# Routing three batches of a mixture-of-experts layer in one pass instead of one batch at a time

## What is computed

```python
scores = sigmoid(x @ gate_weight.T)                    # 16 experts a token
biased = scores + expert_bias
group_scores = top_k(biased.reshape(T, 4, 4), 2).sum(-1)
_, gidx = top_k(group_scores, 2)                       # two of four groups stay
masked = where(group stays, biased, -inf)
_, sel = top_k(masked, 4)                              # four experts a token
w = take(scores, sel); w = w / (w.sum() + 1e-20) * 2.5
```

## Time and profile before

| | |
|---|---|
| runs | 1627.82 us median of 3 (1627.33 to 1629.36) |
| profiled execution | 1630.42 us, of it the span of the engines 1628.7 us |
| busy | TensorE 1290.0 us (79%), VectorE 1448.2 (89%), ScalarE 858.0 (53%), GpSimd 877.7 (54%) |
| instructions | 14027 in all, 1484 on VectorE |
| mean granted clock of TensorE | 0.907 of full |
| DMA | 264 MB, mean 162 GB/s |

### The profile page before, as it was taken

How to read it: one execution, slowest core, us unless ns; L and a number is a source line. 1 busy time by engine, 2 the same in 40 slices (tenths; PEclk the granted TensorE clock), 3 DMA queues, 4 the chain that set the end, 5 groups by cost and what they waited for, 6 DMA issues and landing times.

```text
span 1628.7 us, 14027 instructions
## 1 busy us (share of the span) xinstructions
PE 1290.0 (79%) x4244; PEld 710.4 (44%) x4244; DVE 1448.2 (89%) x1484; ACT 858.0 (53%) x1362; POOL 877.7 (54%) x449
## 2 busy tenths in 40 slices
PE   6785786888689868987869998799886998705778
PEld 2321332433244324442527576466664666503444
DVE  4899989999999999998897999999899999957884
ACT  5754647563755475444854765457564444414441
POOL 0467656645655565550464456755567665566521
PEclk8898799899989998998979999899999999957889
DMA  7354444434543454350366677686776777664421
GB/s 243 97 136 118 110 121 136 139 75 132 136 125 78 130 129 116 89 156 28 95 177 201 224 256 274 205 238 232 272 245 210 273 266 269 200 178 118 134 78 52
DMA packets 99836, 264.28 MB, mean 162 GB/s; under 512 B 10832, under 2 KB 11344, under 8 KB 93616
## 3 DMA queue, kind: packets, MB, share of 16 engines
q1 hardware_dynamic: 87936, 225.36, 47.0%
q0 software_dynamic: 11440, 37.50, 6.9%
q10 hardware_dynamic: 384, 0.52, 0.1%
HBM read 233.73 MB, written 29.62 MB: 162 GB/s over the span
## 4 chain that ended last, share of the span: by engine, by line
DVE 23%; PE 17%; issue 9%; DMA 6%; ACT 5%; POOL 4%; SPq 0%; DVEq 0%; ACTq 0%; POOLq 0%
PE banks L1109 7%; DVE state L1606 7%; DVE banks L1598 5%; DMA ys_d<-expert_out 3%; PE banks L1120 3%; DMA expert_w<-in_moe_w 2%; POOL state L442 2%; DVE x_res L1785 2%; DVE y_scan L1617 2%; PE banks L1029 1%; PE banks L1076 1%; DVE du L1327 1%; DVE small L1379 1%; PE banks L1257 1%; PE banks L1088 1%
## 5 line engine op out<-in xcount | busy, mean ns | idle before, releaser
L442 POOL TENSOR_TENSOR state<-state,bc_rows 128x1024 f32<-128x1024 f32 x256 | 606.5, 2370 | 620.8 <-DVE banks L1598 620.6
L1029 PE MATMUL banks<-state,ident 128*128 128x512 f32 x640 | 356.6, 691 | 132.7 <-POOL state L442 132.4
L1606 DVE TENSOR_TENSOR_SCAN state<-decay,banks 128x1024 f32<-128x1024 f32 x176 | 402.1, 2285 | 15.5 <-PE banks L1029 10.8
L1598 DVE TENSOR_TENSOR banks<-du,bc_rows 128x1024 f32<-128x1024 f32 x256 | 352.4, 1377 | 14.8 <-DVE state L1606 0.6
L1109 PE MATMUL banks<-z_gate,expert_w 128*128 128x256 f32 (+1 forms) x1504 | 287.2, 349 | 10.0 <-DMA expert_w<-in_moe_w 6.2
L1109 PEld LDWEIGHTS banks<-z_gate,expert_w 128*128 128x128 f32 x1504 | 250.8, 192 | 65.3 <-issue 24.3
L684 ACT ACTIVATE decay<-delta,neg_a 128x511 f32<-128x511 f32 x352 | 231.5, 713 | 89.0 <-DVE state L1606 77.7
L1029 PEld LDWEIGHTS banks<-state,ident 128*128 128x128 f32 x640 | 125.7, 212 | 335.2 <-POOL state L442 218.3
L1606 DVE TENSOR_TENSOR_SCAN state<-expert_w,banks 128x1024 f32<-128x1024 f32 x80 | 182.9, 2286 | 7.9 <-ACT expert_w L684 5.2
L1120 PE MATMUL banks<-expert_w,hidden 128*128 128x512 f32 x316 | 157.4, 614 | 3.1 <-DVE hidden L1627 3.1
L1617 DVE TENSOR_TENSOR y_scan<-y_scan,state 128x1024 f32<-128x1024 f32 x96 | 136.3, 1420 | 11.8 <-POOL state L442 11.6
(11 more groups left out here) (253 smaller groups left out, 1718.8 us busy)
## 6 DMA issues: line engine op xcount, KB each, us to landing
bc_rows<-bc_d SPq DMA_DIRECT2D x208, 512.0 KB
expert_w<-in_moe_w SPq DMA_DIRECT2D x48, 1536.0 KB, 9.2
ys_d<-expert_out SPq DMA_DIRECT2D x32, 512.0 KB, 10.2
ctx_t<-in_ctxT SPq DMA_DIRECT2D x8, 512.0 KB, 6.6
x_res<-in_x SPq DMA_DIRECT2D x4, 1024.0 KB, 10.7
xn_d<-y_scan SPq DMA_DIRECT2D x4, 1024.0 KB, 7.4
ys_d<-expert_out SPq DMA_DIRECT2D x15, 256.0 KB, 9.6
out_x<-x_res SPq DMA_DIRECT2D x3, 1024.0 KB, 4.4
```

The source lines that it names most:

```text
L442: nc.gpsimd.tensor_tensor(W[:, c % 4], W[:, c % 4], bcast2(BC[:, u, 1, :]), ALU.mult).then_inc(mulc_done, 1)
L1029: mm = nc.tensor.matmul(PS[:, m], ID[:, :], W[:, c % 4, m, :], start=False, stop=True, skip_group_check=True)
L1598: nc.vector.tensor_tensor(drive(s), DU[:, s % 2, 2 * h:2 * h + 2, :], bcast2(BC[:, u, 0, :]), ALU.mult).then_inc(mulb_done, 1)
L1606: nc.vector.tensor_tensor_scan(flat(W[:, c % 4]), flat(DAS[c % da_slots(s, i)]), flat(drive(s)), 0.0, ALU.mult, ALU.add).then_inc(scan_don ...
```

## The change

Batches 0, 1 and 2 are no longer routed one each in stages 1, 2 and 3. They are routed together in stage 3, at the place where batch 2 was routed, on rows of 3 x 64 = 192 columns. Batch 3 is routed where it was.

- `route_exp` writes its result into the batch's part of the weights' tile `CW`, where it waits; the tile `SC` is gone, and `route` computes the weights in place.
- `route(b0, b1, work, rank1, rank2)` takes a range of batches and its work area. For the three batches this is 7 rows of 192 columns in `ZS[:, 0:3]`, the ranks in halves of `ZS[:, 3]`; for batch 3 it is `SM`, `T1` and `T2` as before. It counts `ranked` up by the number of batches.
- Each operation is as it was with three times the columns; only `MAX8`, one for each token group, is issued 12 times instead of 4.
- In `mul_c` the flag `routed` is set for unit 5 of the last turn of stage 3 alone: in stages 1 and 2 multiply 5 waits for `mul_b` 6 again.
- `norm_bias(2 * s)` moves from behind unit 5 (behind the route) to behind unit 6, in all of stages 0 to 3.

```diff
-                routed = 1 <= s < NB and i == TURNS - 1 and c == 5 or s == NB and k + 1 == HS * NB + 2 * HPT
+                routed = s == NB - 1 and i == TURNS - 1 and c == 5 or s == NB and k + 1 == HS * NB + 2 * HPT
...
-                nc.scalar.activation(SC[:, :, :], AUX[0][:, 0:QT * NE].rearrange("p (q e) -> p q e", e=NE), ACT.Exp,
-                                     scale=-1.0).then_inc(sc_ready, 1)
+                nc.scalar.activation(CW[:, f * QT:(f + 1) * QT, :], AUX[0][:, 0:QT * NE].rearrange("p (q e) -> p q e", e=NE),
+                                     ACT.Exp, scale=-1.0).then_inc(sc_ready, 1)
...
-            def route(b):
-                q16 = lambda i: SM[:, i, :].rearrange("p (q e) -> p q e", e=NE)
-                dve.wait_ge(sc_ready, b + 1)
+            def route(b0, b1, work, rank1, rank2):
+
+                nq = QT * (b1 - b0)
+                n, gn = nq * NE, nq * NGRP
+                row = lambda i, m=n, at=0: work[:, i * n + at:i * n + at + m]
+                q16 = lambda i: row(i).rearrange("p (q e) -> p q e", e=NE)
+                sel, cw = (v[:, b0 * QT:b1 * QT, :] for v in (SEL, CW))
+                dve.wait_ge(sc_ready, b1)
                 dve.wait_ge(ld_small, 16 * 4)
 
-                link(nc.vector.tensor_scalar(SC[:, :, :], SC[:, :, :], 1.0, None, ALU.add))
-                link(nc.vector.reciprocal(SC[:, :, :], SC[:, :, :]))
+                link(nc.vector.tensor_scalar(cw, cw, 1.0, None, ALU.add))
+                link(nc.vector.reciprocal(cw, cw))
...
-                largest = SM[:, 1, 0:QT * 8].rearrange("p (q n) -> p q n", n=8)
-                for q in range(QT):
+
+                largest = row(1, nq * 8).rearrange("p (q n) -> p q n", n=8)
+                for q in range(nq):
                     ins = nc.vector.max(out=largest[:, q, :], in_=masked[:, q, :])
...
-                nc.vector.tensor_tensor(cw, cw, tot.unsqueeze(2).to_broadcast([P, QT, NE]), ALU.mult).then_inc(ranked, 1)
+                nc.vector.tensor_tensor(cw, cw, tot.unsqueeze(2).to_broadcast([P, nq, NE]), ALU.mult).then_inc(ranked, b1 - b0)
...
-                    if c == 5:
-                        if f >= 0:
-                            route(f)
+                    if c == 5 and s == NB - 1:
+
+                        route(0, s, flat(ZS[:, 0:3]), ZS[:, 3, 0:L // 2], ZS[:, 3, L // 2:])
+                    if c == 6:
                         norm_bias(2 * s)
                     if c == 6 and f >= 0:
                         shared_hidden(f, 0)
...
-            route(f)
+            route(f, s, flat(SM[:, :, :]), T1, T2)
```

More of the change, by code:

```diff
@@ L1410, in norm_bias, with rank_of @@
                                                op1=ALU.mult).then_inc(zn_ready, 1)
[L1412 to L1417, removed]
+            def rank_of(out, m, n, tri, s1, s2, nq=QT):
+                a = s1[:, 0:nq * n * n].rearrange("p (q e f) -> p q e f", q=nq, e=n)
+                c = s2[:, 0:nq * n * n].rearrange("p (q e f) -> p q e f", q=nq, e=n)
+                other = m.unsqueeze(2).to_broadcast([P, nq, n, n])
+                own = m.unsqueeze(3).to_broadcast([P, nq, n, n])
@@ L1418, in rank_of @@
                 nc.vector.tensor_tensor(a, other, own, ALU.is_gt)
                 link(nc.vector.tensor_tensor(c, other, own, ALU.is_equal))
-                link(nc.vector.tensor_tensor(c, c, tri.unsqueeze(1).to_broadcast([P, QT, n, n]), ALU.mult))
+                link(nc.vector.tensor_tensor(c, c, tri.unsqueeze(1).to_broadcast([P, nq, n, n]), ALU.mult))
                 link(nc.vector.tensor_tensor(a, a, c, ALU.add))
                 link(nc.vector.reduce_sum(out, a, AX.X))
-            def route(b):
-                q16 = lambda i: SM[:, i, :].rearrange("p (q e) -> p q e", e=NE)
-                dve.wait_ge(sc_ready, b + 1)
+            def route(b0, b1, work, rank1, rank2):
[5 more added lines that the diff above has]
+                dve.wait_ge(sc_ready, b1)
@@ L1435, in route @@
-                mx, mn = SM[:, 1, 0:32], SM[:, 2, 0:32]
+                link(nc.vector.tensor_tensor(biased, cw, EB[:, :].unsqueeze(1).to_broadcast([P, nq, NE]), ALU.add))
+                pairs = row(0).rearrange("p (n two) -> p n two", two=2)
+                mx, mn = row(1, n // 2), row(2, n // 2)
                 nc.vector.tensor_tensor(mx, pairs[:, :, 0], pairs[:, :, 1], ALU.max)
@@ L1438, in route @@
                 mxp, mnp = [v.rearrange("p (n two) -> p n two", two=2) for v in (mx, mn)]
-                top, lo, hi2 = SM[:, 3, 0:16], SM[:, 3, 16:32], SM[:, 3, 32:48]
+                top, lo, hi2 = row(3, gn), row(3, gn, gn), row(3, gn, 2 * gn)
                 nc.vector.tensor_tensor(top, mxp[:, :, 0], mxp[:, :, 1], ALU.max)
@@ L1467, in route @@
                 nc.vector.memset(starts[:, :, 0:1], 0.0)
-                many = SM[:, 1, 32:32 + QT]
+                many = row(1, nq, nq * 8)
                 link(nc.vector.reduce_sum(many, over, AX.X))
-                link(nc.vector.tensor_tensor_scan(SM[:, 5, :], SM[:, 4, :], SM[:, 3, :], 0.0, ALU.mult, ALU.add))
-                link(nc.vector.tensor_tensor(q16(5), q16(5), many.unsqueeze(2).to_broadcast([P, QT, NE]), ALU.add))
+                link(nc.vector.tensor_tensor_scan(row(5), row(4), row(3), 0.0, ALU.mult, ALU.add))
+                link(nc.vector.tensor_tensor(q16(5), q16(5), many.unsqueeze(2).to_broadcast([P, nq, NE]), ALU.add))
                 link(nc.vector.scalar_tensor_tensor(out=equal, in0=q16(5), scalar=float(TOPK), in1=equal, op0=ALU.is_le,
@@ L1474, in route @@
                 link(nc.vector.tensor_tensor(sel, over, equal, ALU.add))
-                link(nc.vector.tensor_tensor(cw, SC[:, :, :], sel, ALU.mult))
-                tot = SM[:, 6, 0:QT]
+                link(nc.vector.tensor_tensor(cw, cw, sel, ALU.mult))
+                tot = row(6, nq)
                 link(nc.vector.reduce_sum(tot, cw, AX.X))
```

19 lines of the change are left out of this document (7 added, 12 removed).

## The result

| | before | after |
|---|---|---|
| median of 6 runs each | 1629.47 us | 1616.12 us |
| lowest to highest | 1627.33 to 1631.12 | 1613.93 to 1621.30 |
| profiled execution, its span | 1630.42, 1628.7 | 1617.39, 1615.7 |
| busy share of VectorE, TensorE | 89%, 79% | 89%, 80% |

The ratio of the runs is 0.9923 (95% interval 0.9906 to 0.994): 12.5 us or 0.8% faster. The same kernel measured once more, on another chip, gave 0.9908 (0.9884 to 0.9932), 1616.51 us. Forecast were 1616.8 us and 11.0 us of gain.

The account below looks back on a forecast made before the run. VectorE (89% busy) was taken to set the pace inside a stage, TensorE's gaps behind VectorE's L1635 and its slow clock the transitions: -6.6 - 8.4 + 3.7 + 0.3 = -11.0 us, so 1616.8 us, range 1612.5 to 1622.

Parts of the forecast that it names:

- Stage 1, -6.6 forecast: Stage 1 to scan 4 of the next: TensorE gains gaps of 4.02 and 0.87 us and 1.7 us of slow L1068.
- stage 2, -8.4: Stage 2 to scan 4 of the next: TensorE gains its 5.40 us gap and 3.0 us of slow L1068.
- L1635 then needs the port ... ends at 322.9: Stage 1, VectorE: L1635 waits for GpSimd's multiply 5 and delta sum, ending at 322.9 instead of 332.4, gaining 9.5 us.
- VectorE waits 5.5 us at scan 4: Scan 4 behind stage 1: VectorE, ahead of TensorE, waits about 5.5 us instead of 2.58; 3.8 behind stage 2.
- rival (a): Stages 1 and 2: VectorE decides, not TensorE; both transitions give the whole 9.5 us, 1612.8 us in all; chance 0.07.
- ScalarE: Between route and scan 4: z_gate and taps come early enough, 3.8 us of cover; ScalarE as releaser would show the forecast wrong.
- Stage 3, route +3.7: Stage 3, VectorE: one route of 192 columns instead of 64 costs 3.7 us, all on the path to L1635.
- Stage 3, clock +0.3: Stage 3, TensorE: the slow stretch behind the longer gap costs 0.3 us more, range -0.4 to +1.5.
- rival (e): Stage 3: work per column makes the wide route thrice as long, +13 us; 1627 us in all; chance 0.02.
- TensorE's gap there, 11 us: Stage 3, behind the wide route: TensorE's gap before the second L1068 grows from 7.39 to 11.1 us.
- The clock in stages 1 and 2: Second L1068 in stages 1 and 2: without a gap TensorE runs at the full clock, about 7.1 us.
- norm_bias, the flag, the row loads at 0: Later norm_bias, multiply 5 waiting again in stages 1 and 2, and SP's row loads without the pause: each costs nothing.

Follow-up runs that it names:

- e9: The changed kernel (after) measured once more, unchanged, on a second chip; median 1616.51 us, ratio to before 0.9908.
- e1: After plus eight linked memsets on VectorE behind unit 5 of the last turn in stages 1 and 2, 4.0 us put in; 1622.74 us, one run.
- e2: After plus eighteen linked memsets on VectorE behind unit 5 of the last turn in stages 1 and 2, 9.2 us put in; 1631.39 us, one run.
- e11: After with only batch 2 routed in stage 3, batches 0 and 1 routed in stage 4 ahead of the last; 1617.16 us, one run.
- e12: After plus eight linked memsets (4.05 us) on VectorE directly behind the wide route of stage 3; 1618.37 us, one run.
- e8: After with the delay of e1 and GpSimd's second delta sum moved from behind its multiply 6 to behind multiply 7; 1622.38 us, one run.
- e3: After with all four batches routed at once in stage 4 on 256 columns, none in stage 3; 1605.29 us, ratio to before 0.987.
- e6: After with norm_bias back behind unit 5 in stages 0 to 3; 1621.22 us, one run.
- e7: After with GpSimd's multiply 5 freed of its wait in stages 1 and 2, as before the change; 1619.37 us, one run.
- e5: After plus ten matmuls with a zeroed operand on TensorE behind sum_state 5 of stage 3, to fill its gap; 1614.22 us, one run.

## Why the prediction was right, step by step

- **Stage 1, -6.6 forecast, -7.09 measured; stage 2, -8.4 and -8.75.** The gap closed, the slow part went (7.03 us; forecast 7.1), and the wait at L1076 went. In stage 1 L1067 begins 332.55 - 328.33 = 4.22 us earlier where the idle time was 4.02, and L1075 7.02 us earlier. That the sum of both stages comes out (15.0 forecast, 15.8 measured) has its reason: before the change TensorE's idle time and slow part are the amount by which the stretch exceeds its gapless work, and after the change that work is what ends last. That the stages match one by one is luck. Both profiled executions had the slow clock in stage 1 and the fast one in stage 2; against e9 the two gains are 8.5 and 7.2. Over the seven traces in the table of levels the sum is 14.3 to 16.1.
- **"L1635 then needs the port ... ends at 322.9": wrong.** It ended at 321.99 (321.30 + 0.69), beside a delta sum of GpSimd that ran from 319.84 to 322.20. It reads one operand from PSUM. The multiply behind it, with two SBUF operands, took 1.38 us instead of 1.23. So VectorE gained 10.4 us at this step (332.40 to 321.99), not 9.5. It changed nothing, as TensorE ended last. The Trainium skill's GPSIMD Engine Reference (specification table) names instructions with two SBUF inputs; I had stretched it to one with one, and the row agrees with the page, not with me.
- **"VectorE waits 5.5 us at scan 4" and 3.8: measured 4.71 and 4.21.** Sizes near, meaning wrong, though the difference that the prediction itself worked out for stage 1 (VectorE 2.9 us ahead) is near the cover measured. I read the 2.58 us before the change as proof that TensorE is last, and held it against rival (a). But that wait is there also when VectorE's L1637 decides (e1, e2, e11, e12, stage 1 of e8, stage 3 of e3): from L1637 the way leads through L1075, L958, L1021 and L1028 on TensorE to scan 4, and in all of these is 2.58 or 2.59 us longer than VectorE's own. The cover is the wait less 2.58: 2.1 and 1.6 us, with 1.02 for ScalarE in the first. Had VectorE gained some 3 us less in stage 1, or 1.6 in stage 2, it would have decided there, as in rival (a).
- **ScalarE.** It does appear as a releaser, 1.02 us at scan 0, which I had named as a sign of being wrong. It is harmless: part of the cover that the delays used up, and it is there only where TensorE's clock was low ahead of it (not in stage 2 of after, not in stage 1 of e9). The taps began at 332.24 (forecast 332.3) and held up nothing.
- **Stage 3, route +3.7: measured +3.66.** The terms held too: L1434 1.35 us (forecast 0.553 + 128 x 0.00625 = 1.35), the twelve MAX8 1.02 (0.40 + 0.64 = 1.04), the scan 0.56 (0.292 + 0.27), 192 columns of tensor_tensor 0.36 (0.225 + 0.133). The vanished growth at the head held as well.
- **Stage 3, clock +0.3: measured 0**, and the step was wrong in kind: TensorE is not last there. L1067 took 9.82 us in one execution and 8.92 in another of the same kernel, with 56.87 and 56.85 us for the whole stretch.
- **Slips in the working.** The stated bounds of route and clock (2.7 to 5, -0.4 to +1.5) give 1615.1 to 1619.3, not 1614.5 to 1619.5, and rival (e)'s -15.0 + 13 + 0.3 gives 1626, not 1627. Neither touches the forecast.
- **TensorE's gap there, 11 us:** 9.25 in one execution, 11.11 in the other. It depends on how late TensorE reaches it, and costs nothing either way.
- **The clock in stages 1 and 2:** without a gap the granted clock was 1.00 at the second L1067 (windows at the end), against 0.70 in the earlier trace rows for stage 2. The Trainium skill, TensorE: Matmul & The Clock Gate (Part 1), calls the half clock the default that activity releases; these rows agree.
- **norm_bias, the flag, the row loads at 0:** e6, e7 and e11 for the first two; no DMA is a releaser between route and scan 4 in after's rows (no run tests the row loads).

The three terms make -12.1 where -11.0 was forecast; the rest up to 12.5 or 13.4 lies within what runs differ by.

## What to carry to other kernels

A wait at the place where two engines meet is not slack. Before counting it as cover, look at the same place in a stretch where the other engine certainly decides: what is left of the wait there is a constant of the order written out (2.58 us here), and only what exceeds it is cover. A delay of a known size on the suspected engine measures this in one run: what does not arrive is the cover, at the clock that the other engine had in the execution compared with. So compare with a second execution before calling two covers different: here 3.1 and 1.6 us changed places between two traces of one kernel. And batching pays by the chains that go away, not by the columns: in stage 3 the wider route cost all of its 3.66 us, while dropping the route there altogether took 12.49 us off that stretch and cost 4.0 in stage 4, 7.7 us by the medians.

## What the runs showed of the hardware

- After idle time TensorE's L1067 was slow without order in how long it rested: 8.80 us behind 2.62 us of rest (e5, at a mean granted clock of 0.81, between the levels of 1.2 and 2.4 GHz), 8.82 behind 5.67 (e11), 9.82 behind 9.25, 8.92 behind 11.11, 8.53 behind 15.31 (e12, at 0.83). A short rest can do it and need not: in e8 L1075 stands behind 2.29 us of rest in both stages and took 3.70 us in stage 1, but 5.40 us in stage 2, where the granted clock was 1.00 ahead of the rest and 0.68 behind it. In after, windows of busy time by engine, then granted clock, DMA share and GB/s:

```profile
638.70:648.40 9.70, 9.69 (x17) 4.21 (x18) 9.60 (x5) 7.66 (x12) 8.54 (x3) 0.72 0.20 54
328.30:335.30 7.00, 7.00 (x18) 3.14 (x17) 5.81 (x4) 6.30 (x10) 4.40 (x3) 1.00 0.25 81
```

- Where TensorE decides, its clock moves the stage as a whole: the stretch of stage 1 took 46.04 us in one execution of after and 44.59 in the other, that of stage 2 44.57 and 46.15, with a granted clock of 0.80 ahead of the long ones and 0.89 ahead of the short. Where VectorE decides, stage 3, the two agree within 0.02. A single execution can therefore mislead by 1.5 us a stage on the one kind of stretch, and not on the other.
- VectorE's reciprocal costs 1.35 us at 192 columns and 1.75 at 256, against 0.553 at 64: about 6.25 ns a column throughout.
